# Query and key projections in halves of 512 and 384 tokens, smaller first pieces, and a last tile finished in two halves side by side

## The chip, the cores and the metric

The kernel runs on one core of a Trainium2 chip. The metric is the device time of one execution in microseconds (us), lower is better. The kernel before took 524.78 us (median of 3 runs, 523.88 to 526.72).

## What is computed

One decoder layer on x (8 batches x 112 tokens x 1024 features), in float32: self-attention with 16 heads, cross-attention to a context of 375 rows for each batch, and a linear layer with a low-rank part chosen by batch, each followed by a residual sum and a layer norm.

```python
def reference(x, ctx_4096, Wq, Wk, Wv, Wo, weight, bias, lora_A, lora_B, starts):
    # self-attention: q, k rotated by position, causal mask, softmax, heads of 64
    q, k, v = x @ Wq, x @ Wk, x @ Wv
    x = _layernorm(x + attention(rotary(q), rotary(k), v) @ Wo)
    # cross-attention: one head over the 1024 features
    e = softmax(einsum('bqd,bkd->bqk', x, ctx_4096))
    x = _layernorm(x + einsum('bqk,bkd->bqd', e, ctx_4096))
    # linear layer with a low-rank addition for some batches
    y = einsum('bsd,od->bso', x, weight) + bias
    lo = einsum('bsr,bor->bso', einsum('bsd,brd->bsr', x, A), Bw)
    return _layernorm(x + y + where(use_lora, lo, 0))
```

## The kernel before

The 896 tokens (8 x 112) are seven tiles of 128; the features are eight tiles of 128 (index k). Every large product is made of three: each operand is split into a rounded part (`_hi`, by ScalarE) and the rest (`_lo`, by VectorE or GpSimd), and hi x hi, hi x lo and lo x hi are added up in PSUM. Every engine has one program, written out by hand in order; semaphores tie them together (`then_inc`, `wait_ge`). SyncE (SP) issues nearly all DMAs, in the order of its program.

The stages, in the order of TensorE's program:
- Warm-up: VectorE fills `warm` with ones (L1280), and TensorE multiplies it `WARM_UP` = 4 times (L608). Each of these float32 products stands in the trace as two records.
- Values: L611 to L630. For each k, seven products x_hi x wv_hi, seven x_hi x wv_lo and seven x_lo x wv_hi, one of each for a tile of tokens (L547), into one PSUM bank for each tile. For k = 0 the input comes in pieces: x_feat in columns 0 to 512 and 512 to 896 (L316, L317), the weights from ScalarE's queue (L910). ScalarE rounds x's first piece, the weights, and x's second piece (L979 to L981), VectorE makes the rests (L1292 to L1294).
- Query and key projections with the self-attention: `step` (L584) for each of eight pairs of heads. `project_part` (L534) multiplies the weights of one k (stationary, 128 x 128) with x (moving) for one half h of the tokens, columns 448 h to 448 h + 448, into `PROD[h]`; `project` runs over k. In one step: four k of the query's first half, the scores of the pair before (`score`), its mix with the values (`mix_heads`), the other four k, the query's second half, the key's first half, the key's second half. VectorE's `keep_qk` (L1320) takes each half out of PSUM, four batches at a time, with the rotation's factor (`turn`), and raises `qk_kept`. Between these it masks scores, takes maxima, transposes probabilities (`turn_prob`) and makes rests.
- The output projection `wo`, the cross-attention and the linear layer `ffn` (products of L651, L737, L768 to L773), interleaved tile by tile.
- The normalisations: VectorE measures (`bn_stats`, `bn_aggr`), then `centre` (L1427) writes the variance plus epsilon and the negated mean, each raising `var_set`; GpSimd's `power` (L1738) waits for both, takes the power -0.5 (`rstd_set`), and multiplies it with the negated mean (`shift_set`).
- The end, for the last tile: VectorE measures columns 512 to 1024 straight from PSUM (`measure_y(6, 1)`), GpSimd runs `power`, then VectorE finishes columns 512 to 1024 (L1706) after `rstd_set`, and ScalarE columns 0 to 512 (L1274) after `shift_set`. SyncE stores the two halves one after the other (L522 to L525).

Of the kernel before, what the change touches and what calls it, by code (L numbers as in the profile page):

```python
# [10 lines left out]
ALU = mybir.AluOpType  # L11
ACT = mybir.ActivationFunctionType
AX = mybir.AxisListType

P = 128
# [18 lines left out]
MASKED = -2e9  # L34
WARM_UP = 4
SCORE_SCALE = 1.0 / (2.0 * HD ** 0.5)
# [20 lines left out]
CT_HI = 5  # L57
T_RING = 3
QUAD = 32
QUADS = P // QUAD  # L60
# [47 lines left out]
def tile_of(i):  # L108
    return slice(i * P, i * P + P)
# [13 lines left out]
def build(nc, x_feat, x_tok, qkv_w, wo_w, ffn_w, ctx_feat, ctx_tok, starts, rotary, causal,  # L123
          identity, route, out):
    st = ExitStack()
    with st:
# [3 lines left out]
        def sem(name):  # L130
            return st.enter_context(nc.semaphore(name))
# [110 lines left out]
        wv_in = [[sem(f"wv_in{c}_{k}") for k in range(KT)] for c in range(2)]  # L242
        wv_rounded, wv_rest = sem("wv_rounded"), sem("wv_rest")
        v_done, v_kept = sem("v_done"), sem("v_kept")
        v_in = [sem(f"v_in{c}") for c in range(2)]
# [36 lines left out]
        y_kept, y_stats, y_ready = sem("y_kept"), sem("y_stats"), sem("y_ready")  # L282
        last_ready = [sem(f"last_ready{n}") for n in range(2)]
        y_out = [sem(f"y_out{i}") for i in range(4)]
# [28 lines left out]
        def _(sp):  # L313
            def load_x_feat(k):
                if k == 0:
                    sp.dma_start(x_raw[:, k, 0:HALF], x_feat[:, k, 0:HALF]).then_inc(x_in[k], 16)  # L316
                    sp.dma_start(x_raw[:, k, HALF:B * S], x_feat[:, k, HALF:B * S]  # L317
                                 ).then_inc(x_tail_in, 16)
                else:
                    sp.dma_start(x_raw[:, k, :], x_feat[:, k, :]).then_inc(x_in[k], 16)  # L320
# [200 lines left out]
            i = TILES - 1  # L521
            for n in range(2):  # L522
                sp.wait_ge(last_ready[1 - n], 1)
                cols = slice(HALF * (1 - n), HALF * (1 - n) + HALF)
                sp.dma_start(out_rows[tile_of(i), cols], y_t[i % 4][:, cols]).then_inc(y_out[i % 4], 16)  # L525
            sp.wait_ge(y_out[0], 16 * 2)
# [6 lines left out]
        def _(pe):  # L533
            def project_part(k, w, h, to):  # L534
                for a, b in ((w_hi[w], x_hi), (w_hi[w], x_lo), (w_lo[w], x_hi)):
                    last = pe.matmul(to[:, 0:HT], a[:, k, :], b[:, k, HT * h:HT * h + HT],  # L536
                                     start=(k == 0 and b is x_hi and a is w_hi[w]),
                                     stop=(k == KT - 1 and a is w_lo[w]))
                return last
# [71 lines left out]
            for k in range(KT):  # L611
                pe.wait_ge(x_rounded, k + 2 if k else 1)
                pe.wait_ge(wv_rounded, k + 1)
                for i in range(TILES):
                    if k == 0 and i == HALF // P:
                        pe.wait_ge(x_rounded, 2)
                    value_part(0, k, i, x_hi, wv_hi)
# [291 lines left out]
        def _(act):  # L909
# [68 lines left out]

            round_x(0, slice(0, HALF))  # L979
            round_wv(0, 0)  # L980
            round_x(0, slice(HALF, B * S))  # L981
            for k in range(1, KT):
# [118 lines left out]
            def norm_y(i):  # L1101
# [170 lines left out]
            i = TILES - 1  # L1272
            act.wait_ge(shift_set[2], i + 1)
            act.activation(y_t[i % 4][:, 0:HALF], y_t[i % 4][:, 0:HALF], ACT.Identity,  # L1274
                           bias=norm[2][:, i, 5:6], scale=norm[2][:, i, 4:5]).then_inc(last_ready[0], 1)


        @block.vector
        def _(dve):
# [7 lines left out]
            def rest_x(k, cols=slice(0, B * S)):  # L1287
                dve.wait_ge(x_rounded, k + 2 if k or cols.start else 1)
                dve.tensor_tensor(x_lo[:, k, cols], x_raw[:, k, cols],
                                  x_hi[:, k, cols].bitcast(F32), ALU.subtract).then_inc(x_rest, 1)  # L1290

            rest_wv(0, 0)  # L1292
            rest_x(0, slice(0, HALF))
            rest_x(0, slice(HALF, B * S))  # L1294
            for k in range(1, KT):
# [20 lines left out]

            scale = turn[:, :].unsqueeze(1).broadcast_to([P, HB, S])
            hidden = mask[:, :].unsqueeze(1).broadcast_to([S, HB, S])

            def keep_qk(u, w, h, done, frm):  # L1320
                dve.wait_ge(proj_done, done)
                dve.tensor_tensor(qk[u][w][:, HB * h:HB * h + HB, :],  # L1322
                                  frm[:, 0:HT].rearrange("p (b s) -> p b s", b=HB),
                                  scale, ALU.mult).then_inc(qk_kept, 1)

# [224 lines left out]
            for g in range(3):  # L1550
# [155 lines left out]
            dve.tensor_scalar(y_t[i % 4][:, HALF:D], GROUP[2 * WO - 1][:, :], norm[2][:, i, 0:1],  # L1706
                              norm[2][:, i, 4:5], ALU.subtract, ALU.mult).then_inc(last_ready[1], 1)


        @block.gpsimd  # L1710
        def _(pool):
# [26 lines left out]
            def power(which, i, width):  # L1738
                v = norm[which][0:width, i, :]
                pool.wait_ge(var_set[which], 2 * i + 2)  # L1740
                pool.tensor_tensor(v[:, 4:5], v[:, 2:3], minus_half[0:width, :],  # L1741
                                   ALU.pow).then_inc(rstd_set[which], 1)
                pool.wait_ge(rstd_set[which], i + 1)
                pool.tensor_tensor(v[:, 5:6], v[:, 3:4], v[:, 4:5],
                                   ALU.mult).then_inc(shift_set[which], 1)
# [144 lines left out]
```

## Time and profile before

| | |
|---|---|
| median of 3 runs | 524.78 us (523.88 to 526.72) |
| profiled execution | 525.95 us |
| its span, first to last instruction | 524.2 us |
| mean granted TensorE clock | 0.997 of full speed |
| busy: TensorE products / weight loads | 515.3 us / 444.7 us |
| busy: VectorE / ScalarE / GpSimd | 320.3 / 261.7 / 152.2 us |
| bytes moved by DMA | 65.60 MB, mean 125 GB/s |

PE is TensorE's products, PEld its weight loads (they overlap), DVE is VectorE, ACT ScalarE, POOL GpSimd, SP SyncE. The span of a row is in microseconds from the first instruction. A product's recorded duration overlaps the next product, so the distance of two starts is what one costs in a stream. The granted clock tells at which of its two levels, 1.2 or 2.4 GHz, TensorE runs.

### The profile page before, as it was taken

The page shows a single profiled execution, that of the slowest core. Times are in us where ns is not written, and L with a number is a line of the kernel's source. Part 1 is how long each engine was busy: PE and PEld are TensorE (multiplying, and loading weights), DVE is VectorE, ACT ScalarE, POOL GpSimd, SP SyncE. Part 2 cuts the span into 40 slices and gives each one's busy share as a digit, 9 for nine tenths or more (in the row PEclk, how much of TensorE's full clock was granted, in tenths as well). Part 3 has the DMA queues.
Part 4 walks back from the last instruction along what each step waited for, and adds up shares of the span by engine and source line. Part 5 has one row for each costly group of instructions (what it writes and reads, how often), then busy time and mean ns, then how long its engine had stood idle before and what let it go on. Part 6 is the DMA issues. An engine that isn't in the chain of part 4 may idle for free.

```text
span 524.2 us, 7773 instructions
## 1 busy us (share of the span) xinstructions
PE 515.3 (98%) x2868; PEld 444.7 (85%) x2868; DVE 320.3 (61%) x660; ACT 261.7 (50%) x663; POOL 152.2 (29%) x139
## 2 busy tenths in 40 slices
PE   8999999999999999999999999999998999999995
PEld 5888888999999999999978888888887888988884
DVE  4832000177776868677674797779987776845432
ACT  5713210173846648384565356357777464525231
POOL 0003600436353554642006250114946010110010
PEclk9999999999999999999999999999999999999998
DMA  9906712331112111100087577579986466433011
GB/s 285 314 16 167 195 40 81 107 136 41 41 48 75 42 40 43 41 1 1 1 257 183 138 207 211 148 198 265 274 243 193 126 194 225 109 87 111 2 75 47
DMA packets 37958, 65.60 MB, mean 125 GB/s; under 512 B 4872, under 2 KB 20616, under 8 KB 37920
## 3 DMA queue, kind: packets, MB, share of 16 engines
q1 hardware_dynamic: 37392, 64.84, 42.9%
q8 instruction: 23, 0.38, 0.3%
q10 hardware_dynamic: 528, 0.26, 0.2%
q14 instruction: 15, 0.12, 0.1%
HBM read 54.08 MB, written 3.67 MB: 110 GB/s over the span
## 4 chain that ended last, share of the span: by engine, by line
PE 97%; DVE 2%; issue 0%; ACT 0%; POOL 0%; POOLq 0%; DVEq 0%
PE bank L536 30%; PE bank L651 29%; PE bank L547 15%; PE bank L737 6%; PE bank L563 3%; PE bank L578 3%; PE bank L770 2%; PE bank L768 2%; PE bank L773 2%; PE bank L721 1%; PE bank L609 1%; PE bank L710 1%; PE bank L682 1%; PE bank L684 1%; DVE cf_lo L1506 1%; PE bank L752 0%
## 5 line engine op out<-in xcount | busy, mean ns | idle before, releaser
L536 PE MATMUL bank<-x_hi,w_hi 128*128 128x448 f32 x256 | 94.3, 368 | 0.0
L536 PE MATMUL bank<-x_hi,w_lo 128*128 128x448 f32 x256 | 93.5, 365 | 0.0
L536 PE MATMUL bank<-x_lo,w_hi 128*128 128x448 f32 x256 | 93.5, 365 | 0.0
L1359 DVE STREAM_TRANSPOSE prob_t<-prob 32x256 f32<-32x256 f32 x160 | 69.7, 436 | 13.0 <-ACT prob L942 10.3
L651 PE MATMUL bank<-wo,act_hi 128*128 128x512 f32 x224 | 70.2, 395 | 0.0
L651 PE MATMUL bank<-ffn,act_hi 128*128 128x512 f32 x224 | 69.9, 393 | 0.0
L1728 POOL TENSOR_TENSOR w_lo<-w_mix,w_hi 128x1024 fp32r<-128x1024 f32 x16 | 38.2, 2389 | 105.2 <-ACT w_hi L917 105.2
L932 ACT ACTIVATE prob<-prob,shift 112x112 f32<-112x112 f32 x128 | 47.8, 375 | 38.9 <-DVE shift L1342 38.9
L1741 POOL TENSOR_TENSOR norm<-norm,minus_half 128x1 f32<-128x1 f32 (+1 forms) x22 | 16.6, 754 | 159.9 <-DVE norm L1432 159.9
L536 PEld LDWEIGHTS bank<-x_hi,w_hi 128*128 128x128 f32 x256 | 48.1, 188 | 4.7
L536 PEld LDWEIGHTS bank<-x_hi,w_lo 128*128 128x128 f32 x256 | 48.1, 188 | 3.8
L536 PEld LDWEIGHTS bank<-x_lo,w_hi 128*128 128x128 f32 x256 | 48.1, 188 | 3.7
L651 PEld LDWEIGHTS bank<-wo,act_hi 128*128 128x128 f32 x224 | 41.3, 188 | 8.7
L651 PEld LDWEIGHTS bank<-ffn,act_hi 128*128 128x128 f32 x224 | 41.2, 188 | 8.1
L1028 ACT ACTIVATE ct_hi<-ct_raw 125x512 fp32r<-125x512 f32 x48 | 28.8, 625 | 33.2 <-DMA ct_raw<-ctx_tok 19.8
L917 ACT ACTIVATE w_hi<-w_mix 128x1024 fp32r<-128x1024 f32 x16 | 16.9, 1054 | 54.8 <-PE bank L536 47.0
L651 PE MATMUL bank<-wo,act_lo 128*128 128x512 f32 x112 | 43.7, 390 | 0.0
L651 PE MATMUL bank<-ffn,act_lo 128*128 128x512 f32 x112 | 43.7, 390 | 0.0
L1506 DVE TENSOR_TENSOR cf_lo<-cf_raw,cf_hi 128x752 fp32r<-128x752 f32 x32 | 34.3, 1081 | 7.8 <-ACT cf_hi L1016 7.6
L942 ACT ACTIVATE prob<-prob,inv 112x112 f32<-112x112 f32 x128 | 37.3, 375 | 0.1
L1322 DVE TENSOR_TENSOR q_feat<-bank,turn 128x448 f32<-128x448 f32 x16 | 9.9, 619 | 43.4 <-PE bank L536 43.3
L1499 DVE TENSOR_TENSOR ct_lo<-ct_raw,ct_hi 125x512 fp32r<-125x512 f32 x48 | 32.9, 719 | 5.4 <-ACT ct_hi L1028 5.1
(114 smaller groups left out, 984.1 us busy)
## 6 DMA issues: line engine op xcount, KB each, us to landing
cf_raw<-ctx_feat SPq DMA_DIRECT2D x32, 376.0 KB, 4.3
ct_raw<-ctx_tok SPq DMA_DIRECT2D x24, 448.0 KB
w_raw<-qkv_w SPq DMA_DIRECT2D x16, 512.0 KB, 3.4
half_raw<-wo_w SPq DMA_DIRECT2D x16, 256.0 KB, 6.0
half_raw<-ffn_w SPq DMA_DIRECT2D x16, 256.0 KB, 6.1
wv_raw<-qkv_w SPq DMA_DIRECT2D x15, 256.0 KB, 7.5
x_raw<-x_feat SPq DMA_DIRECT2D x7, 448.0 KB, 8.2
out<-y_t SPq DMA_DIRECT2D x6, 512.0 KB, 3.6
```

What stands on the lines that cost most here:

```text
L536: last = pe.matmul(to[:, 0:HT], a[:, k, :], b[:, k, HT * h:HT * h + HT], start=(k == 0 and b is x_hi and a is w_hi[w]), stop=(k == KT - 1 ...
L547: return pe.matmul(value_bank(c, i)[:, :], a[:, k, tile_of(i)], w[c][:, k, :], start=(k == 0 and a is x_hi and w is wv_hi), stop=(k == KT ...
L651: last = pe.matmul(to[:, :], a[:, k, cols], weight(of, n, k, w), start=(k == 0 and a is act_hi and w == 0), stop=(ends and k == KT - 1 and ...
L737: last = pe.matmul(CSCORE[0:S, 0:LKP], a[:, k, tokens_of(b)], c[slot][:, kk, :], start=(k == 0 and a is act_hi and c is cf_hi), stop=(k == ...
L917: act.activation(w_hi[w][:, :, :], w_mix[:, :, :], ACT.Copy).then_inc(w_rounded, 1)
L932: last = act.activation(prob[a][:, b, :], prob[a][:, b, :], ACT.Exp, bias=shift[:, a, b:b + 1], accum_out=total[:, a, b:b + 1])
L942: last = act.activation(prob[a][:, b, :], prob[a][:, b, :], ACT.Copy, scale=inv[:, a, b:b + 1])
L1028: act.activation(ct_hi[m % CT_HI][:, :], ct_raw[c][:, HALF * n:HALF * n + HALF], ACT.Copy).then_inc(ct_rounded, 1)
L1359: return dve.transpose(quads(prob_t_wide[r], key, query), quads(prob_wide[r], query, key))
L1499: dve.tensor_tensor(ct_lo[c][:, cols], ct_raw[c][:, cols], ct_hi[m % CT_HI][:, :].bitcast(F32), ALU.subtract).then_inc(ct_rest[n], 1)
L1506: dve.tensor_tensor(cf_lo[slot][:, :, :], cf_raw[slot][:, :, :], cf_hi[slot][:, :, :].bitcast(F32), ALU.subtract).then_inc(cf_rest, 1)
L1728: pool.tensor_tensor(w_lo[w][:, :, :], w_mix[:, :, :], w_hi[w][:, :, :].bitcast(F32), ALU.subtract).then_inc(w_rest, 1)
```

## The change

It has three parts.
1. `project_part` splits the tokens at SPLIT = 512 instead of 448: the first half is 512 columns wide, the second 384. As 512 is four batches and 64 tokens, `keep_qk` uses two instructions for a half: one for the part of batch 4 that the half holds (64 or 48 columns), one for the whole batches (4 or 3).
2. `WARM_UP` is 2. The first load of x is split at FIRST = 256 tokens instead of 512. ScalarE rounds columns 0 to 256 of the first piece of value weights, VectorE copies columns 256 to 512 with the same rounding (`wv_tail_rounded`), and TensorE waits for both.
3. In the last tile ScalarE centres columns 0 to 512 as soon as the negated mean is there, scales them after `rstd_set`, and issues their store from its own queue; SyncE stores columns 512 to 1024. In every normalisation `power` starts its first instruction after the variance, and waits for the negated mean only ahead of the second.

```diff
-WARM_UP = 4
+WARM_UP = 2
+FIRST = 2 * P
+SPLIT = HB * S + 64
...
-                    sp.dma_start(x_raw[:, k, 0:HALF], x_feat[:, k, 0:HALF]).then_inc(x_in[k], 16)
-                    sp.dma_start(x_raw[:, k, HALF:B * S], x_feat[:, k, HALF:B * S]
+                    sp.dma_start(x_raw[:, k, 0:FIRST], x_feat[:, k, 0:FIRST]).then_inc(x_in[k], 16)
+                    sp.dma_start(x_raw[:, k, FIRST:B * S], x_feat[:, k, FIRST:B * S]
...
-            for n in range(2):
-                sp.wait_ge(last_ready[1 - n], 1)
-                cols = slice(HALF * (1 - n), HALF * (1 - n) + HALF)
-                sp.dma_start(out_rows[tile_of(i), cols], y_t[i % 4][:, cols]).then_inc(y_out[i % 4], 16)
+            sp.wait_ge(last_ready, 1)
+            sp.dma_start(out_rows[tile_of(i), HALF:D], y_t[i % 4][:, HALF:D]).then_inc(y_out[i % 4], 16)
...
             def project_part(k, w, h, to):
+                cols = slice(SPLIT * h, SPLIT + (B * S - SPLIT) * h)
                 for a, b in ((w_hi[w], x_hi), (w_hi[w], x_lo), (w_lo[w], x_hi)):
-                    last = pe.matmul(to[:, 0:HT], a[:, k, :], b[:, k, HT * h:HT * h + HT],
+                    last = pe.matmul(to[:, 0:cols.stop - cols.start], a[:, k, :], b[:, k, cols],
...
                 pe.wait_ge(wv_rounded, k + 1)
+                if k == 0:
+                    pe.wait_ge(wv_tail_rounded, 1)
                 for i in range(TILES):
-                    if k == 0 and i == HALF // P:
+                    if k == 0 and i == FIRST // P:
                         pe.wait_ge(x_rounded, 2)
...
-            round_x(0, slice(0, HALF))
-            round_wv(0, 0)
-            round_x(0, slice(HALF, B * S))
+            round_x(0, slice(0, FIRST))
+            act.wait_ge(wv_in[0][0], 16)
+            act.activation(wv_hi[0][:, 0, 0:FIRST], wv_raw[0][:, 0, 0:FIRST],
+                           ACT.Copy).then_inc(wv_rounded, 1)
+            round_x(0, slice(FIRST, B * S))
...
-            act.wait_ge(shift_set[2], i + 1)
+            act.wait_ge(var_set[2], 2 * i + 2)
             act.activation(y_t[i % 4][:, 0:HALF], y_t[i % 4][:, 0:HALF], ACT.Identity,
-                           bias=norm[2][:, i, 5:6], scale=norm[2][:, i, 4:5]).then_inc(last_ready[0], 1)
+                           bias=norm[2][:, i, 3:4], scale=1.0).then_inc(last_centred, 1)
+            act.wait_ge(rstd_set[2], i + 1)
+            act.wait_ge(last_centred, 1)
+            act.activation(y_t[i % 4][:, 0:HALF], y_t[i % 4][:, 0:HALF], ACT.Copy,
+                           scale=norm[2][:, i, 4:5]).then_inc(last_scaled, 1)
+            act.wait_ge(last_scaled, 1)
+            act.dma_start(out_rows[tile_of(i), 0:HALF], y_t[i % 4][:, 0:HALF]).then_inc(y_out[i % 4], 16)
...
+            dve.wait_ge(wv_in[0][0], 16)
+            dve.tensor_copy(wv_hi[0][:, 0, FIRST:HALF], wv_raw[0][:, 0, FIRST:HALF]
+                            ).then_inc(wv_tail_rounded, 1)
+            dve.wait_ge(wv_tail_rounded, 1)
             rest_wv(0, 0)
-            rest_x(0, slice(0, HALF))
-            rest_x(0, slice(HALF, B * S))
+            rest_x(0, slice(0, FIRST))
+            rest_x(0, slice(FIRST, B * S))
...
             def keep_qk(u, w, h, done, frm):
                 dve.wait_ge(proj_done, done)
-                dve.tensor_tensor(qk[u][w][:, HB * h:HB * h + HB, :],
-                                  frm[:, 0:HT].rearrange("p (b s) -> p b s", b=HB),
-                                  scale, ALU.mult).then_inc(qk_kept, 1)
+                first = SPLIT - HT
+                if h == 0:
+                    whole, at_whole = slice(0, HB), 0
+                    some, at_some = slice(0, first), HT
+                else:
+                    whole, at_whole = slice(HB + 1, B), S - first
+                    some, at_some = slice(first, S), 0
+                n, m = whole.stop - whole.start, some.stop - some.start
+                dve.tensor_tensor(qk[u][w][:, HB, some], frm[:, at_some:at_some + m],
+                                  turn[:, some], ALU.mult)
+                dve.tensor_tensor(qk[u][w][:, whole, :],
+                                  frm[:, at_whole:at_whole + n * S].rearrange("p (b s) -> p b s", b=n),
+                                  turn[:, :].unsqueeze(1).broadcast_to([P, n, S]),
+                                  ALU.mult).then_inc(qk_kept, 1)
...
-                pool.wait_ge(var_set[which], 2 * i + 2)
+                pool.wait_ge(var_set[which], 2 * i + 1)
                 pool.tensor_tensor(v[:, 4:5], v[:, 2:3], minus_half[0:width, :],
                                    ALU.pow).then_inc(rstd_set[which], 1)
+                pool.wait_ge(var_set[which], 2 * i + 2)
                 pool.wait_ge(rstd_set[which], i + 1)
```

## Rows read from the trace of the kernel before

**Rows 1.** The page, busy time, share of the span and instructions of TensorE.

```profile
PE 515.3 (98%) x2868; PEld 444.7 (85%) x2868; DVE 320.3 (61%) x660; ACT 261.7 (50%) x663; POOL 152.2 (29%) x139
```

**Rows 2.** The chain that ended last, from 0 to 20 us: start, length, what.

```profile
1.38 5.47 PE bank L609 x8
```

**Rows 3.** Waits of TensorE, whole span: us in total, times, longest.

```profile
PE bank L682 <- DVE t_both L1530: 1.5, 1, 1.5
```

**Rows 4.** Timeline of TensorE in a projection step: start us, duration, what.

```profile
176.63 0.37 PE L536 MATMUL bank<-x_hi,w_hi 128*128 128x448 f32 x1
...
186.77 0.37 PE L536 MATMUL bank<-x_hi,w_lo 128*128 128x448 f32 x1
```

**Rows 5.** Timeline in the value stage, seven products merged to one row.

```profile
11.50 1.75 PE L547 MATMUL bank<-wv_hi,x_hi 128*128 128x512 f32 x7
...
16.26 1.75 PE L547 MATMUL bank<-wv_hi,x_hi 128*128 128x512 f32 x7
```

**Rows 6.** Timeline of TensorE in the cross scores.

```profile
309.15 0.33 PE L737 MATMUL bank<-cf_hi,act_lo 128*112 128x376 f32 x1
...
312.56 0.33 PE L737 MATMUL bank<-cf_lo,act_hi 128*112 128x376 f32 x1
```

**Rows 7.** Timeline of TensorE in the low-rank products.

```profile
446.32 0.28 PE L791 MATMUL bank<-act_hi,a_both 128*112 128x256 f32 x1
...
447.72 0.28 PE L791 MATMUL bank<-act_hi,a_both 128*112 128x256 f32 x1
```

**Rows 8.** Weight loads by line and shape: busy us, mean ns, idle before.

```profile
L536 PEld LDWEIGHTS bank<-x_hi,w_hi 128*128 128x128 f32 x256 | 48.1, 188 | 4.7
...
L737 PEld LDWEIGHTS bank<-cf_hi,act_hi 128*112 128x112 f32 x64 | 11.2, 174 | 0.3
```

**Rows 9.** Timeline of VectorE at a step's end, and two short instructions.

```profile
193.26 0.62 DVE L1322 TENSOR_TENSOR k_feat<-bank,turn 128x448 f32<-128x448 f32 x1 [1.97 <-PE bank L536]
...
196.66 1.16 DVE L1334 SCALAR_TENSOR_TENSOR prob<-bank,mask 112x448 f32<-112x448 f32 x2 [0.50 <-PE bank L563]
...
404.65 0.47 DVE L1530 SCALAR_TENSOR_TENSOR t_both<-bank,sel,t_both 48x112 fp32r<-48x112 f32 x2
```

**Rows 10.** Timeline of all engines at the start.

```profile
4.53 0.34 PEld L609 LDWEIGHTS bank<-warm 128*128 128x128 f32 x1 [0.41 <-issue]
4.94 0.63 ACT L921 ACTIVATE wv_hi<-wv_raw 128x512 fp32r<-128x512 f32 x1 [0.16 <-DMA wv_raw<-qkv_w]
...
5.28 0.34 PEld L609 LDWEIGHTS bank<-warm 128*128 128x128 f32 x1 [0.41 <-issue]
5.48 0.51 ACT L970 ACTIVATE x_hi<-x_raw 128x384 fp32r<-128x384 f32 x1
...
5.94 0.19 PEld L609 LDWEIGHTS bank<-warm 128*128 128x128 f32 x1 [0.32 <-issue]
...
6.69 1.34 PEld L547 LDWEIGHTS bank<-wv_hi,x_hi 128*128 128x128 f32 x6 [0.19 <-issue]
...
9.01 0.62 ACT L921 ACTIVATE wv_hi<-wv_raw 128x512 fp32r<-128x512 f32 x1
```

**Rows 11.** Timeline of the other engines behind the last product.

```profile
519.18 0.15 DVE L1431 TENSOR_SCALAR norm<-norm 128x1 f32<-128x1 f32 x1
519.25 0.14 DVE L1432 TENSOR_SCALAR norm<-norm 128x1 f32<-128x1 f32 x1
519.47 0.55 POOL L1741 TENSOR_TENSOR norm<-norm,minus_half 128x1 f32<-128x1 f32 x1 [11.65 <-DVE norm L1432]
520.06 0.81 DVE L1706 TENSOR_SCALAR y_t<-bank,norm 128x512 f32<-128x512 f32 x1 [0.66 <-POOL norm L1741]
...
520.33 0.81 ACT L1274 ACTIVATE y_t<-y_t,norm 128x512 f32<-128x512 f32 x1 [7.42 <-POOL norm L1744]
520.89 0.81 SPq L525 DMA_DIRECT2D out<-y_t  x2
```

**Rows 12.** DMA issues from 505 us on: KB each, median us to landing.

```profile
out<-y_t SPq DMA_DIRECT2D x2, 256.0 KB, 2.2
```

More of the change, by code:

```diff
@@ L243, in build @@
         wv_rounded, wv_rest = sem("wv_rounded"), sem("wv_rest")
+        wv_tail_rounded = sem("wv_tail_rounded")
         v_done, v_kept = sem("v_done"), sem("v_kept")
@@ L282, in build @@
         y_kept, y_stats, y_ready = sem("y_kept"), sem("y_stats"), sem("y_ready")
-        last_ready = [sem(f"last_ready{n}") for n in range(2)]
+        last_centred, last_scaled, last_ready = sem("last_centred"), sem("last_scaled"), sem("last_ready")
         y_out = [sem(f"y_out{i}") for i in range(4)]
@@ L1315, in _ @@
                               ALU.is_equal).then_inc(routed, 1)
-            scale = turn[:, :].unsqueeze(1).broadcast_to([P, HB, S])
             hidden = mask[:, :].unsqueeze(1).broadcast_to([S, HB, S])
@@ L1706, in _ @@
             dve.tensor_scalar(y_t[i % 4][:, HALF:D], GROUP[2 * WO - 1][:, :], norm[2][:, i, 0:1],
-                              norm[2][:, i, 4:5], ALU.subtract, ALU.mult).then_inc(last_ready[1], 1)
+                              norm[2][:, i, 4:5], ALU.subtract, ALU.mult).then_inc(last_ready, 1)
         @block.gpsimd
```

## The prediction

> **What bounds the kernel now.** I read the busy table of the page first: TensorE is busy 98% of the span [rows 1]. The chain of work that ended last says the same in order of time: it is TensorE from its first warm-up product at 1.38 us [rows 2] up to the end, where VectorE's last statistics follow it. The table of waits names one stall of TensorE after the start, 1.5 us for VectorE in the feed-forward part [rows 3]. So a change shortens the kernel by what it takes off TensorE's own stream, by what it takes off the start ahead of that stream, and by what it takes off the chain behind it. Everything else is cover. The profiled execution took 525.95 us (span 524.2 and 1.75 around it), 1.2 us over the median of the runs, 524.78; I sum on the profile and subtract the result from the median.
>
> **Part 1, the projections.** The number of products stays 768: 8 pairs of heads x 2 matrices x 8 feature tiles x 3 products x 2 halves. Before, both halves are 448 tokens wide; after, 384 products are 512 wide and 384 are 384 wide. The columns in all are the same, so the question is how the spacing of two products depends on the width. The traced duration of one product (365 ns) overlaps its neighbour, so I take starts. 448 wide: 50 products from 176.63 to 186.77 us, 202.8 ns each [rows 4]. 512 wide, same 128-column weights: 21 products from 11.50 to 16.26 us, 226.7 ns each [rows 5]. 376 wide, weights of 112 columns: 20 from 309.15 to 312.56 us, 170.5 ns each [rows 6]. 256 wide, weights of 64 and 112 columns in turn: 12 from 446.32 to 447.72 us, 116.7 ns each [rows 7].
>
> Per column that is 0.448 ns from 256 to 376, 0.449 ns from 376 to 448, and only 0.373 ns from 448 to 512. The line bends at the top: the last 64 columns are cheaper than the ones before. A 384-wide product isn't in the trace; its nearest row is the 376-wide one, so I take 170.5 + 8 x 0.449 = 174.1 ns. A pair then costs 226.7 + 174.1 = 400.8 ns instead of 2 x 202.8 = 405.6 ns, and 384 pairs give 384 x -4.8 ns = **-1.8 us**. Bounds: if 384 columns cost their share of 512 (170.0 ns) the term is -3.4 us. If the slope of 0.373 also holds below 448, 384 columns cost 178.9 ns and the term is 0. Above nothing there is the weight load: its record lasts 188 ns for 128 columns and 174 ns for 112 [rows 8]. If the next product had to wait for the end of that record, a 384-wide one would be spaced at 188 ns at least, 384 x +9.1 ns = +3.5 us, and at up to the 202.8 ns of now, +9.2 us. Against such a floor: the 376-wide products run at 170.5 ns though their weight load is recorded with 174 ns, and the 256-wide ones at 116.7 ns with loads of up to 112 columns [rows 6, 7]. So the record holds latency that overlaps, and 16 more weight columns, 14 ns more, don't make a floor of 188.
>
> The Trainium skill speaks against this gain. TensorE: Matmul & The Clock Gate, Back-to-back issue gap, has a gap of N columns at 2.4 GHz plus about 2.5 ns, the weights loading meanwhile; by that the pair costs 378.4 ns both ways and part 1 is worth nothing. The trace is above it at each width (202.8 and 226.7 ns against 189.2 and 215.8), by 13.6 ns at 448 and 10.9 ns at 512.
>
> Moved with it: VectorE now keeps each half with two instructions, for 448 + 64 and 48 + 336 columns, the short ones some 0.24 us (nearest: 48x112, two in 0.47 us) [rows 9]. There are 32 short ones, and as each of the 16 pairs of halves goes from 2 x 0.62 to about 1.5 us, VectorE has 16 x 0.3 = 5 us more. Cover: VectorE is idle 1.97 us before the last keep of a step, and 0.50 us before the masking of the next scores [rows 9]; the latter is the tight one. There the second half is now the narrow one (0.7 us against 0.62), and TensorE's twelve products ahead of the scores are wider (12 x 23.9 ns = 0.29 us later), so the slack grows. TensorE's other waits on a kept half stand a whole half (4.2 us) behind its end. Queued behind a keep on VectorE are the transposes of the probabilities, which come 0.1 us later. I cost all this at nothing; without that cover it is 0.1 us a step, +0.8 us.
>
> **Part 2, the start.** Before, TensorE doesn't get to the first value product at its readiness. ScalarE rounds the first weight piece from 4.94 us for 0.63 us, so its data are there at 5.57, but eight warm-up records (two per product) hold the engine: the chain passes to the value products at 1.38 + 5.47 = 6.85 us [rows 2, 10]. The records are 0.75 us apart while the clock is at its lower level (1.2 GHz, weight load 0.34 us), the one of 5.28 us comes 0.66 us before the next and the one of 5.94 us has a load of 0.19 us: the clock rose at about 5.85 us, to 2.4 GHz [rows 10]. After: four records, so TensorE is free at about 4.55 us. Rounding costs 0.63 us for 512 columns and 0.51 for 384 [rows 10], so 0.39 us for 256; ScalarE's half is ready at 4.94 + 0.39 = 5.33 and VectorE copies the other half beside it (its nearest row is 0.62 us for 448 columns [rows 9], so an estimate of 0.3 to 0.5 us for 256 and an end at 5.3 to 5.4). Products start at about 5.4 us. Until 5.85 us they run at the lower level, which wastes 0.23 us; 0.16 us is the lag that the chain's 6.85 has too (its weight loads go on from 6.69 [rows 10]). The third token tile needs the rest of x rounded: ScalarE starts it at about 5.4 and needs 0.73 us for 640 columns, 6.15 us, which stalls about 0.1 us. So the take-over of the chain moves to 5.4 + 0.23 + 0.16 + 0.1 = 5.9 us: **-0.95 us**. Next limit: the second feature tile's weights are rounded at 9.01 + 0.62 = 9.63 us [rows 10]; TensorE asks for them after 21 products, at about 10.5 us, so 0.9 us of cover remain. The first load in two other pieces (256 and 640 columns for 512 and 384) moves the same bytes, and what lands last ahead of TensorE is the weight piece, which is as before. Bounds: -1.3 us if the piece also lands earlier, -0.5 us if VectorE's copy is late.
>
> The engine is now idle from 4.55 to 5.4 us ahead of the rise of the clock. No row shows whether the rise still comes at 5.85 then; that is rival C.
>
> **Part 3, the end.** Behind the last product stand VectorE's statistics, two small instructions, GpSimd's power (0.55 us) and product, then both engines' half of the last tile, and two stores of SyncE, 0.41 us apart [rows 11]. Now: ScalarE's half is ready at 520.33 + 0.81 = 521.14, its store issued at about 521.3 us and landed 2.2 us later [rows 11, 12]. After: GpSimd starts on the first small instruction (end 519.33 for 519.39, -0.07 us). ScalarE centres from 519.45 to 520.26, beside the power, and scales with 0.81 us from 520.3 to 521.1; its store goes out on its own queue at 521.15. VectorE's half ends at 520.80 and SyncE stores it at once. The later issue moves from 521.3 to 521.15: **-0.15 us**. Bounds: -0.4 us if scaling alone is shorter, +0.3 us if a store from ScalarE's queue lands later than one from SyncE's. The earlier power in the other normalisations is off TensorE's path: nothing.
>
> Sum: -1.8 - 0.95 - 0.15 = -2.9 us: 523.05 us for the profiled execution, **521.9 us** for the median (0.55% less).
>
> **The rivals.**
> A, forecast, 0.55: as summed, 521.9 us; with the bounds of its terms all at once (-3.4 to 0, -1.3 to -0.5, -0.4 to +0.3) 519.7 to 524.6 us.
> B, 0.15: the widths are worth nothing, because cost is linear from 384 to 512 columns; the skill's gap rule ends here too. For it: the slope of 0.373 is the only one measured with 128-column weights at both ends. Against it: two other intervals agree on 0.449. Only the start and end remain, -1.1 us: 523.7 us.
> C, 0.17: the clock rises later, because the engine is idle ahead of it. For it: in the trace the rise came after 4.5 us of unbroken work. Against: only 0.85 us are idle, and TensorE is at work again when the rise was. If the break makes the count begin anew, the rise comes 4.5 us after 5.4, at 9.9 instead of 5.85 us; 4.05 us at half speed cost 2.0 us: -2.9 + 2.0 = -0.9 us, 523.9 us. The Trainium skill (TensorE: Matmul & The Clock Gate, The HAM clock gate) says that the lower level is the default and that sustained activity releases it; what a short break does there, no row of this case shows.
> D, the slower side, 0.09: the weight load sets a floor under the narrow products. It decides from a floor of 181.8 ns on (at 178.9 ns part 1 is even, and 2.9 ns more, 384 times, eat the 1.1 us of parts 2 and 3). At 188 ns the sum is +3.5 - 1.1 = +2.4 us, 527.2 us; at 202.8 ns +9.2 - 1.1 = +8.1 us, 532.9 us.
> E, 0.04: the gain of the first parts is lost again where TensorE waits 1.5 us for VectorE [rows 3]. The wait ends a run of VectorE work that itself begins when TensorE's cross products of batch 3 end (add_row waits for them), so it should move along with TensorE. If the wait grew by half its length, 0.8 us would go, and if by its length 1.5 us: 522.7 to 523.4 us.
>
> **Range and chances.** About 0.5% (2.6 us) is what a measurement of this kernel can tell from no change; the forecast is just beyond it. A lies beyond with seven tenths of its chance (0.39) and inside with the rest; B, C and E lie inside but for some scatter of the measurement, and D lies inside at a floor of 188 ns (527.2 us is 0.46% more) and beyond it above. So: faster by over 0.5% 0.41, within 0.5% 0.52, slower 0.07. The range reaches from A's low bounds taken nearly together, 520.3 us, over B, C and E with their scatter, to 524.9 us, and leaves out D and what is beyond A's low end.
>
> **What the profile after would show.** Part 1: starts of 384-wide products 174 ns apart (B: 179; D: 188 or more) and of 512-wide ones 227 ns, and a step (48 pairs) 0.23 us shorter; VectorE's idle time before the masking not under 0.5 us, no new wait of TensorE on the kept halves. Part 2: four warm-up records, the first value product at 5.4 us, the second feature tile's at 10.5 us instead of 11.50; the change of spacing from 0.43 to 0.23 us tells when the clock rose, and C is right if that is later than 6 us. Part 3: the store of ScalarE's queue at 521.15 on the old time axis. What would make this wrong: a 384-wide spacing away from 174 ns, a late rise of the clock, or a new wait in the projection steps.

## The result, and the profile after

The kernel after takes 523.08 us (median of 22 runs, 522.11 to 527.09) against 525.07 us for the kernel before in the same sessions (22 runs). The two medians differ by 2.0 us. The ratio of the two kernels is 0.9968, with a 95% interval from 0.9957 to 0.9979; by it, the kernel takes 1.7 us less, between 1.1 and 2.3. The forecast was 2.9 us less, 521.9 us, with a range of 520.3 to 524.9 us.

The profiled execution of after took 522.58 us, its span is 520.6 us. That is 3.6 us below the span of before, nearly twice the difference of the medians, so the two traces alone mislead; e1 below shows by how much. The page of after, its span and busy times (compare rows 1):

```profile
span 520.6 us, 7823 instructions
...
PE 513.0 (99%) x2864; PEld 438.4 (84%) x2864; DVE 319.8 (61%) x693; ACT 262.6 (50%) x664; POOL 152.1 (29%) x139
```

Four product records less (two warm-up products), 33 VectorE instructions more. The start, from the timeline of all engines of after (compare rows 10):

```profile
1.38 3.36 PE L612 MATMUL bank<-warm 128*128 128x448 f32 x4 [1.38 <-DVE warm L1293]
...
3.18 0.42 ACT L975 ACTIVATE x_hi<-x_raw 128x256 fp32r<-128x256 f32 x1 [0.67 <-DMA x_raw<-x_feat]
...
3.97 0.42 ACT L986 ACTIVATE wv_hi<-wv_raw 128x256 fp32r<-128x256 f32 x1 [0.38 <-DMA wv_raw<-qkv_w]
3.97 0.29 DVE L1306 CAST wv_hi<-wv_raw 128x256 fp32r<-128x256 f32 x1 [2.65 <-DMA wv_raw<-qkv_w]
...
4.49 0.84 PE L550 MATMUL bank<-wv_hi,x_hi 128*128 128x512 f32 x2
...
4.79 0.74 ACT L975 ACTIVATE x_hi<-x_raw 128x640 fp32r<-128x640 f32 x1 [0.40 <-DMA x_raw<-x_feat]
...
5.58 1.43 PE L550 MATMUL bank<-wv_hi,x_hi 128*128 128x512 f32 x5 [0.25 <-ACT x_hi L975]
...
10.01 1.75 PE L550 MATMUL bank<-wv_hi,x_hi 128*128 128x512 f32 x7
```

The first value product starts at 4.49 us, not at the forecast 5.4, because the weight piece itself is there at 3.97 instead of 4.94 us. TensorE waits 0.25 us for the rest of x; the forecast had 0.1. The second feature tile begins at 10.01 us instead of 11.50 [rows 5].

The projections, from TensorE's timeline in the third step, two places where the width changes (compare rows 4):

```profile
131.18 0.33 PE L539 MATMUL bank<-x_hi,w_hi 128*128 128x384 f32 x1
...
132.25 0.34 PE L539 MATMUL bank<-x_hi,w_hi 128*128 128x384 f32 x1
...
133.11 0.33 PE L539 MATMUL bank<-x_hi,w_lo 128*128 128x384 f32 x1
...
135.19 0.33 PE L539 MATMUL bank<-x_hi,w_lo 128*128 128x384 f32 x1
135.37 0.39 PE L539 MATMUL bank<-x_hi,w_hi 128*128 128x512 f32 x1
...
137.45 0.39 PE L539 MATMUL bank<-x_hi,w_hi 128*128 128x512 f32 x1
137.67 0.39 PE L539 MATMUL bank<-x_lo,w_hi 128*128 128x512 f32 x1
...
140.39 0.39 PE L539 MATMUL bank<-x_lo,w_hi 128*128 128x512 f32 x1
```

A settled narrow stream costs (135.19 - 133.11) / 12 = 173.3 ns a product, a settled wide one (140.39 - 137.67) / 12 = 226.7 ns. But the first six behind a change to 384 columns cost (132.25 - 131.18) / 6 = 178 ns, and the first nine behind a change to 512 cost (137.45 - 135.37) / 9 = 231 ns. Over the stage the means are 174.4 and 228.9 ns, 403.3 ns a pair against 405.3 before. Left out of these means are 14 spacings in each kernel (292 to 310 ns before, 317 to 339 ns after), where TensorE passes from a projection to the scores or goes on after them. The whole stage, from the first product of the projections to the first of the output projection, runs from 81.41 to 260.07 us:

```profile
81.41 0.39 PE L539 MATMUL bank<-x_hi,w_hi 128*128 128x512 f32 x1
...
260.07 0.63 PE L656 MATMUL bank<-wo,act_hi 128*128 128x512 f32 x2
```

That is 178.66 us; before, the same two records stand at 82.90 and 262.36 us, 179.46. In nanoseconds the differences are 178,652 and 179,459, and each of the other traces with the same widths and order repeats its number to the nanosecond (e2, e7, e8, e10 and e12 the one of after; e1, e3, e4 and e9 the one of before). So this stage is worth 0.81 us, and nothing of it is scatter.

VectorE's cover held. The end of a step in its timeline (compare rows 9):

```profile
191.25 0.21 DVE L1346 TENSOR_TENSOR k_feat<-bank,turn 128x48 f32<-128x48 f32 x1 [1.15 <-PE bank L539]
191.37 0.50 DVE L1348 TENSOR_TENSOR k_feat<-bank,turn 128x336 f32<-128x336 f32 x1
191.90 2.24 DVE L1386 STREAM_TRANSPOSE prob_t<-prob 32x256 f32<-32x256 f32 x5
194.97 1.16 DVE L1361 SCALAR_TENSOR_TENSOR prob<-bank,mask 112x448 f32<-112x448 f32 x2 [0.83 <-PE bank L566]
```

The idle time before the masking grew from 0.50 to 0.83 us. All keeps together take 22.0 us instead of 19.9, 2.1 us more, where the prediction had 5.

### The profile page after: what moved, and what is told of

It is laid out like the page before. It is cut to its first block, busy times and chain, and to the rows that moved or that the text cites. A ratio compares the mean times of both kernels' runs of the same rounds, so it can differ in the third digit from the quotient of the medians.

```text
span 520.6 us, 7823 instructions
## 1 busy us (share of the span) xinstructions
PE 513.0 (99%) x2864; PEld 438.4 (84%) x2864; DVE 319.8 (61%) x693; ACT 262.6 (50%) x664; POOL 152.1 (29%) x139
## 4 chain that ended last, share of the span: by engine, by line
PE 98%; DMA 1%; ACT 0%; DVE 0%; SPq 0%; issue 0%; ACTq 0%
PE bank L539 30%; PE bank L656 30%; PE bank L550 15%; PE bank L742 6%; PE bank L566 3%; PE bank L581 3%; PE bank L773 2%; PE bank L775 2%; PE bank L778 2%; PE bank L726 1%; PE bank L715 1%; DMA x_raw<-x_feat 1%; PE bank L687 1%; PE bank L793 1%; PE bank L689 1%; PE bank L796 1%
## 5 line engine op out<-in xcount | busy, mean ns | idle before, releaser
L539 PE MATMUL bank<-x_hi,w_hi 128*128 128x512 f32 (+1 forms) x256 | 93.7, 366 | 0.0
L539 PE MATMUL bank<-x_hi,w_lo 128*128 128x512 f32 (+1 forms) x256 | 93.2, 364 | 0.0
L539 PE MATMUL bank<-x_lo,w_hi 128*128 128x512 f32 (+1 forms) x256 | 93.1, 364 | 0.0
L550 PE MATMUL bank<-wv_hi,x_hi 128*128 128x512 f32 x112 | 36.3, 393 | 0.2 <-ACT x_hi L975 0.2
L1533 DVE TENSOR_TENSOR cf_lo<-cf_raw,cf_hi 128x752 fp32r<-128x752 f32 x32 | 30.9, 979 | 8.1 <-ACT cf_hi L1023 8.1
```

The lines of the kernel that those rows point to most:

```text
L539: last = pe.matmul(to[:, 0:cols.stop - cols.start], a[:, k, :], b[:, k, cols], start=(k == 0 and b is x_hi and a is w_hi[w]), stop=(k == K ...
L550: return pe.matmul(value_bank(c, i)[:, :], a[:, k, tile_of(i)], w[c][:, k, :], start=(k == 0 and a is x_hi and w is wv_hi), stop=(k == KT ...
L1533: dve.tensor_tensor(cf_lo[slot][:, :, :], cf_raw[slot][:, :, :], cf_hi[slot][:, :, :].bitcast(F32), ALU.subtract).then_inc(cf_rest, 1)
```

## The experiments

Each edit is against the kernel before or after, as named. Ratios are to the kernel before, with their 95% intervals; 0.001 is 0.52 us.

**e1, the kernel before again.** No edit.

> The kernel before once more, for a second trace. In the first one TensorE waited 1.5 us for t_both at 403.6 us, behind one 128x752 subtraction of VectorE (cf_lo) that lasted 3.12 us instead of 0.94, with a GpSimd subtraction running beside it; after the change the wait was gone and TensorE 1.5 us further ahead. Theory 1 (accident of phase between VectorE and GpSimd): the second trace shows another length there, and the 1.5 us are not the change's. Theory 2 (fixed by the program): 3.1 us and a wait of 1.5 us again. Also open: the first weight piece was there at 4.94 us before and at 3.97 after. If that is scatter of the DMA, this trace shows another time than 4.94; if the larger pieces cause it, 4.9 again.

Measured: span 521.9 us, 2.3 us less than the first trace of the same kernel. TensorE has no wait at 403 us, and the subtraction is as short as its kind. Its VectorE row, and GpSimd's rows around it:

```profile
400.07 0.93 DVE L1506 TENSOR_TENSOR cf_lo<-cf_raw,cf_hi 128x752 fp32r<-128x752 f32 x1
...
401.01 2.54 POOL L1757 TENSOR_TENSOR ffn<-half_raw,ffn 128x512 fp32r<-128x512 f32 x2
```

In the first trace of before the order of the two is turned: GpSimd's pair of subtractions starts at 400.36 us, VectorE's at 400.58, and VectorE's lasts 3.12 us. It ends at 403.70 us, 0.80 us after the end of GpSimd's pair (402.90):

```profile
400.36 2.54 POOL L1757 TENSOR_TENSOR ffn<-half_raw,ffn 128x512 fp32r<-128x512 f32 x2
...
400.58 3.12 DVE L1506 TENSOR_TENSOR cf_lo<-cf_raw,cf_hi 128x752 fp32r<-128x752 f32 x1
```

Two later traces, e6 and e12, show a third outcome. This is e6:

```profile
398.58 3.25 POOL L1785 TENSOR_TENSOR ffn<-half_raw,ffn 128x512 fp32r<-128x512 f32 x2
...
398.74 1.93 DVE L1533 TENSOR_TENSOR cf_lo<-cf_raw,cf_hi 128x752 fp32r<-128x752 f32 x1
```

Here VectorE gets in between the two: it ends 0.80 us after GpSimd's first subtraction (399.87), and GpSimd's second takes 2.00 us instead of 1.29. In e12 VectorE's takes 2.08 us, again ending 0.80 us after GpSimd's first, and GpSimd's second 1.99 us. So the one that comes second waits for the end of the other's instruction. The Trainium skill (SBUF — State Buffer, SBUF: two separate sides) says this of a VectorE instruction with two SBUF inputs and a GpSimd instruction that reads SBUF: an exclusive lock on a shared port pair for the whole instruction, no sharing. The traces agree: 0.93 us with VectorE first, 1.93 us behind one subtraction of GpSimd, 3.12 us behind two. Why VectorE gets in between the two in e6 and e12 and not in before and e4 is open. Theory 1 holds: the length is an accident of phase. From the first product of the output projection to the last product of all it is 255.42 us in the first trace of before, 253.73 in e1 and 254.22 in after: 1.2 of the 3.6 us between the two spans lie in a stretch that moves by 1.7 us with no edit at all. The weight piece is rounded from 4.98 us here (4.94 before), so its time isn't scatter of that size.

**e2, the widths alone.** Before, with the projections and keeps of after:

```diff
+SPLIT = HB * S + 64
-                    last = pe.matmul(to[:, 0:HT], a[:, k, :], b[:, k, HT * h:HT * h + HT],
+                    last = pe.matmul(to[:, 0:cols.stop - cols.start], a[:, k, :], b[:, k, cols],
```

> Only the projections in 512 and 384 columns. Prediction on record: -1.8 us. From the trace of after: 384-wide products settle at 173.3 ns and 512-wide ones at 226.7, but the first ten or so behind each change of width or of kind are spaced wider (231 ns on average for the wide ones), so a pair costs 403.3 instead of 405.3 ns: 384 x -2.0 = -0.8 us. Rival: the widths are worth nothing, 0 us.

Measured: 0.9995 (0.9978 to 1.0012), 524.42 us. The time alone can't tell -0.8 us from 0. The trace can: the stage takes 178.65 us again (83.14 to 261.79), 0.81 us less than the two traces of before.

**e3, the start alone.** Before, with the warm-up, pieces and split rounding of after:

```diff
-WARM_UP = 4
+WARM_UP = 2
+FIRST = 2 * P
-            round_x(0, slice(0, HALF))
-            round_wv(0, 0)
+            round_x(0, slice(0, FIRST))
+            act.activation(wv_hi[0][:, 0, 0:FIRST], wv_raw[0][:, 0, 0:FIRST],
+                           ACT.Copy).then_inc(wv_rounded, 1)
```

> Only the start: smaller first pieces, two warm-up products, the weight piece rounded by two engines. Prediction on record -0.95 us; the two traces show -1.48 us up to the second feature tile, of which 0.97 us is an earlier landing of the weight piece. If that landing is the change's, -1.5 us; if it is scatter, -0.9 us; if the clock often rises late, between 0 and -0.5 us with more scatter than before.

Measured: 0.9974 (0.9963 to 0.9986), 1.4 us less (0.7 to 1.9). The weight piece lands early here too:

```profile
3.37 0.42 ACT L974 ACTIVATE x_hi<-x_raw 128x256 fp32r<-128x256 f32 x1 [0.86 <-DMA x_raw<-x_feat]
4.19 0.42 ACT L985 ACTIVATE wv_hi<-wv_raw 128x256 fp32r<-128x256 f32 x1 [0.40 <-DMA wv_raw<-qkv_w]
```

So the landing is the change's: the smaller first piece of x is followed by an earlier weight piece, though that comes from another queue. ScalarE begins on it at 4.87 to 5.25 us in the six traces with the old pieces, and at 3.95 to 4.21 us in the eight with the new ones. The first piece of x itself lands at 4.11 to 4.42 us with the old pieces and at 3.16 to 3.36 us with the new ones, and the weight piece lands 0.73 to 0.84 us behind it in all 14. No run changed the size of the pieces alone, but e7 and e8 rule out the number of warm-up products as the cause.

**e4, the end alone.** Before, with the last tile and `power` of after:

```diff
-            act.wait_ge(shift_set[2], i + 1)
+            act.wait_ge(var_set[2], 2 * i + 2)
+            act.dma_start(out_rows[tile_of(i), 0:HALF], y_t[i % 4][:, 0:HALF]).then_inc(y_out[i % 4], 16)
-                pool.wait_ge(var_set[which], 2 * i + 2)
+                pool.wait_ge(var_set[which], 2 * i + 1)
```

> Only the end: halves side by side, store from ScalarE's queue, power a step earlier. Prediction -0.15 us; the traces show the end of the last half at 3.17 us behind the last product's start against 3.37 before, so -0.2 to -0.3 us. Rival: a store from ScalarE's queue lands later and eats it, 0 us.

Measured: 1.0003 (0.9991 to 1.0015). In the traces the last byte's landing stands 5.75 us behind the start of the last product with the new end (e4 and after) and 5.84 us with the old one (before and e1; e3 has 5.82): 0.09 us less, below what the timing can see. This trace again has the long subtraction (3.35 us) and a wait of 1.7 us for t_both.

**e5, halves of 480 and 416.** Before, with the widths' code and another SPLIT:

```diff
+SPLIT = HB * S + 32
```

> The kernel before with halves of 480 and 416 columns, for their spacing. Theory 1: a settled stream costs the width at 2.4 GHz plus 13.3 ns (512: 226.7, 384: 173.3), and 448 is the odd one that never settles (202.7 instead of 200.0). Then 480 settles at 213.3 ns and 416 at 186.7 ns, 400.0 ns a pair, as 512 and 384 do, each with ten or so wider spacings behind a change. Theory 2: the line bends between 448 and 512 as the prediction had it: 480 at 214.7 and 416 at 188.4 ns, in every spacing.

Measured: from TensorE's timeline of one step:

```profile
135.16 0.35 PE L539 MATMUL bank<-x_hi,w_lo 128*128 128x416 f32 x1
...
137.40 0.35 PE L539 MATMUL bank<-x_hi,w_lo 128*128 128x416 f32 x1
...
139.11 0.38 PE L539 MATMUL bank<-x_lo,w_hi 128*128 128x480 f32 x1
...
142.57 0.38 PE L539 MATMUL bank<-x_hi,w_lo 128*128 128x480 f32 x1
```

2.24 us / 12 = 186.7 ns for 416 columns, 3.46 us / 16 = 216.3 ns for 480 (217.1 on average over the stage). Theory 1 is right for 416 and wrong for 480; theory 2 is wrong for both. Theory 1 also has ten or so wider spacings behind a change of width, and these don't come: the mean of all 384 spacings of 416 columns is 186.8 ns, the settled value. The unsettled spacings are thus seen at 384 and 512 columns, and not at 416. The stage takes 178.92 us, 0.54 us less than with 448.

This trace also shows that the long subtraction isn't the only thing that delays t_both. TensorE waits 1.0 us for it, though VectorE's subtraction takes 0.94 us; VectorE then waits for ScalarE, which itself had waited for a DMA:

```profile
400.52 0.84 ACT L1019 ACTIVATE cf_hi<-cf_raw 128x752 fp32r<-128x752 f32 x1 [1.36 <-DMA cf_raw<-ctx_feat]
...
403.71 0.42 DVE L1529 TENSOR_TENSOR bank<-bank,t_part 48x256 f32<-48x256 f32 x1 [1.38 <-ACT t_part L1089]
```

In e8 it is the same, with a wait of TensorE of 0.8 us.

**e6, narrow behind narrow, wide behind wide.** After, with the key's halves in the other order (their banks, keeps and the scores' wait go with them):

```diff
-                project(1, 0, PROD[0])
+                project(1, 1, PROD[0])
                 pe.wait_ge(qk_kept, 4 * s + 2)
-                project(1, 1, PROD[1])
+                project(1, 0, PROD[1])
```

> The kernel after, with the key's narrow half ahead of its wide half, so that wide follows wide and narrow follows narrow, and the width changes twice a step less. Theory 1: the unsettled spacings behind a change of width are what ate half of the gain: 40 ns behind a change to 512 and 26 ns behind one to 384, 66 ns less in each step, 0.5 us less than after, 0.9958 of before. Theory 2: they follow something else (the start of an accumulation, the kept half), and nothing moves: 0.9968.

Measured: 0.9956 (0.9943 to 0.997), 522.97 us. The stage runs from 81.41 to 259.57 us, 178.16 us: 0.49 us less than after, against 0.5 expected.

```profile
81.41 0.39 PE L539 MATMUL bank<-x_hi,w_hi 128*128 128x512 f32 x1
...
259.57 0.62 PE L656 MATMUL bank<-wo,act_hi 128*128 128x512 f32 x2
```

Theory 1 holds: the unsettled spacings follow the change of width. The evidence is the trace; in time alone the interval overlaps with that of after.

**e7, four warm-up products again.** After, with

```diff
-WARM_UP = 2
+WARM_UP = 4
```

> The kernel after with four warm-up products instead of two. Theory 1: they hold the engine while the operands wait: the first value product goes from 4.5 back to between 5.7 and 6.9 us, according to when the clock rises; 0.9 to 1.2 us more than after, 0.999 of before. Theory 2: the earlier pieces alone make the gain at the start, and it stays at 0.997.

Measured: 0.9976 (0.9963 to 0.9989), 523.9 us. The second feature tile begins at 11.36 us, 1.35 us later than in after, with the clock rising at 5.55 against 4.79 us. In time it is 0.4 us more than after, and the intervals overlap; the direction is theory 1's, the size is smaller than expected, and the time alone doesn't show it. At the second feature tile the earlier pieces without the shorter warm-up bring 0.14 us against before (11.36 for 11.50 us), and the clock's earlier rise in that trace (5.55 for 5.84 us) can account for them. The eight records still hold the engine:

```profile
1.38 5.32 PE L612 MATMUL bank<-warm 128*128 128x448 f32 x8 [1.38 <-DVE warm L1293]
6.20 2.13 PE L550 MATMUL bank<-wv_hi,x_hi 128*128 128x512 f32 x7
```

**e8, no warm-up.** After, with

```diff
-WARM_UP = 2
+WARM_UP = 0
```

> The kernel after without a warm-up. If the rise of the clock wants work before it, it comes later than in any run so far (4.8 to 7.3 us) and the value stage starts at the lower level: up to 1.5 us more than after, 0.999 or so. Rival: the clock rises when it did, and nothing moves, 0.9968.

Measured: 0.9983 (0.9972 to 0.9993), 524.09 us. By the ratios that is 0.8 us more than after, and the intervals overlap a little (0.9972 and 0.9979).

```profile
4.76 3.26 PE L550 MATMUL bank<-wv_hi,x_hi 128*128 128x512 f32 x7 [4.76 <-ACT wv_hi L986]
7.86 1.76 PE L550 MATMUL bank<-wv_lo,x_hi 128*128 128x512 f32 x7
...
11.04 1.75 PE L550 MATMUL bank<-wv_hi,x_hi 128*128 128x512 f32 x7
```

The first seven products take 3.26 us, nearly twice what a settled seven take (1.75): they run at 1.2 GHz. The clock rose at 7.68 us, in this one trace 0.27 us later than in the latest of the others (4.66 to 7.41). The second feature tile begins at 11.04 us, within the range of the traces with two warm-up products (9.99 to 11.10), so this trace doesn't show where the 0.8 us are lost.

**e9 and e10, the masking of the low-rank part ahead of the long subtraction.** Before (e9) and after (e10), with

```diff
             rest_turned("a5")
-            rest_cf(22)
             mask_t(0)
+            rest_cf(22)
```

> The kernel before with VectorE's mask_t(0), for which TensorE waits at 403 us, ahead of the subtraction of the context chunk 22 (which in two traces of four lasted over 2 us beside GpSimd). Theory 1: that wait (0 to 2.1 us, another in each trace) is an accident of phase behind a long subtraction; with the order turned it is gone, the median falls by about 1 us (0.998) and the scatter of the runs shrinks. Theory 2: VectorE's total work up to there sets it, and the wait comes back one place later (cross_score of batch 5 for its chunk): 1.000.

Measured: 0.9996 (0.9984 to 1.0007). In the trace the wait of TensorE for t_both is gone and none has come in its place: the last product starts 253.65 us after the first of the output projection, against 255.42 us in the first trace of before and 253.73 us in e1. The median doesn't fall, and the scatter of the runs doesn't shrink (523.40 to 526.17 us; before 523.67 to 526.34). So neither theory holds as written: the accident is real in a single execution, but the median of before seems to hold little of it.

> The kernel after with the same turned order. Theory 1: 0.5 to 1 us less than after, 0.995 to 0.996 of before, with the ratio to the previous kernel of this call equal to the sum of the parts (start -1.4, widths -0.8, end -0.1 us: 0.9956). Theory 2: as after, 0.9968.

Measured: 0.9972 (0.9961 to 0.9984), 523.5 us; no wait in this trace either. Theory 2: as after.

**e11, both.** The edits of e6 and e10 together.

> The kernel after with both: the key's narrow half first and mask_t(0) first. If the two are independent: after -0.5 us -0.7 us, 0.9945 of before, the fastest so far. If the wider shift only brings other collisions of VectorE with GpSimd: 0.9956, as with the swap alone.

Measured: 0.9954 (0.9941 to 0.9966), 522.11 us, the fastest of the study, and no faster than the swap alone within its interval.

**e12, both stores from SyncE.** After, with

```diff
             sp.dma_start(out_rows[tile_of(i), HALF:D], y_t[i % 4][:, HALF:D]).then_inc(y_out[i % 4], 16)
+            sp.wait_ge(last_scaled, 1)
+            sp.dma_start(out_rows[tile_of(i), 0:HALF], y_t[i % 4][:, 0:HALF]).then_inc(y_out[i % 4], 16)
...
-            act.wait_ge(last_scaled, 1)
-            act.dma_start(out_rows[tile_of(i), 0:HALF], y_t[i % 4][:, 0:HALF]).then_inc(y_out[i % 4], 16)
```

> The kernel after, with both stores of the last tile from SyncE's queue again (the halves still side by side). The store from ScalarE's queue was issued at 517.50 us and landed 2.5 us later, while SyncE's landed 2.0 us after 517.34. Theory 1: ScalarE's queue is the slower one; from SyncE the second store is issued 0.35 us behind the first, at 517.7, and lands after 2.2 us, so the end is the same within 0.1 us. Theory 2: two stores in flight slow one another whatever their queue: the second lands 2.5 us after its issue, and the end comes 0.2 us later.

Measured: the end is where theory 1 has it, but that doesn't make its reason right. The last landing is 5.74 us behind the last product's start, as in after (5.75). The table of DMA issues of after and of e12 (KB each, median us to landing):

```profile
out<-y_t SPq DMA_DIRECT2D x1, 256.0 KB, 2.0
out<-y_t ACTq DMA_DIRECT2D x1, 256.0 KB, 2.5
```

```profile
out<-y_t SPq DMA_DIRECT2D x2, 256.0 KB, 2.2
```

The second store is issued 0.16 us behind the first from ScalarE's queue and takes 2.53 us; from SyncE's queue it is issued 0.38 us behind and takes 2.31 us. Both land 2.69 us after the issue of the first store. In all 14 traces the last landing stands 2.69 to 2.73 us behind that first issue, whatever the queue and the moment of the second. So the end follows the first store, and the queue of the second makes no difference to it; whether a queue is slower in itself, these runs can't tell.

## Why the prediction was right, and which of its terms were off

The time is a sum of four stretches, and the traces give each on its own:

| | forecast | in the traces | timed alone |
|---|---|---|---|
| start, to the second feature tile | -0.95 us | -1.4 us (means of six) | -1.4 (-1.9 to -0.7) |
| projections | -1.8 us | -0.81 us | -0.3 (-1.2 to +0.6) |
| after them, to the last product | 0 | scatter, 253.65 to 255.76 us | |
| behind the last product | -0.15 us | -0.09 us | +0.2 (-0.5 to +0.8) |
| sum | -2.9 us | -2.3 us | |

Sign and range held, and luck had a part in it: the two large terms were off in opposite directions, the projections by 1.0 us too much and the start by 0.5 us too little. The sum of the traces is at the edge of the measured interval (-1.1 to -2.3); the 0.6 us between it and the 1.7 us by the ratio stay open (0.3 us against the medians). Two stretches vary between traces of the same code: the start, with the moment at which the clock rises, and the stretch after the projections, where e9 and e10 didn't settle it.

Part 1, the step that failed: "a pair then costs 226.7 + 174.1". The interpolated 174.1 ns was right (174.4 on average), though for a reason the prediction didn't have. What was mis-sized is the 226.7 ns, which I read from a stream that had been 512 wide for a long time. In a step the width changes four times, and six to nine unsettled spacings follow each change, so the mean is 228.9 ns; 384 x (403.3 - 405.3) = -0.8 us. The trace of before could have warned me: its six spacings of value products from 6.92 to 8.31 us, behind the change from the 448-wide warm-up, are 231 ns each on average, ahead of the settled 226.7. e6 shows the mechanism by taking two of the four changes away: the 0.49 us come back.

Part 2, the step that failed: "what lands last ahead of TensorE is the weight piece, which is as before". It landed 0.97 us earlier, and the bound for that (-1.3 us) was taken too near. The forecast start of the value products, 5.4 us, became 4.49 us in after. The second feature tile begins at 10.36 us on average in the six traces with the new start and two warm-up products (9.99 to 11.10), and at 11.77 us in the six with the old one (10.89 to 12.25). In the same traces the clock rose 0.5 us earlier on average with the new start (5.87 against 6.40 us); at half a microsecond for each, some 0.2 us of the 1.4 us go with that (an estimate), and six traces of each can't tell whether it is chance.

Part 3: right in sign and too small to be timed. The step that failed is "The later issue moves from 521.3 to 521.15". On the time axis of before it moved further, from 521.27 to 520.99 us, but the landing doesn't follow the later issue: it follows the first one, which moved by 0.06 us, from 3.12 to 3.06 us behind the start of the last product. The 2.2 us to landing that the term used is the median of two stores; the later one took 2.34 us, and they are 0.38 us apart, not 0.41.

The rivals.

B (widths worth nothing) falls by the 0.81 us that repeat in every trace. The gap rule of the Trainium skill (TensorE: Matmul & The Clock Gate, Back-to-back issue gap), which the page gives for an isolated product, doesn't describe these streams: 384 columns cost 173.3 ns settled against 162.5 by the rule, and the pair is 5.3 ns cheaper when both are settled, not the same.

C (the clock rises late after the break) wasn't put to the test. Over six traces each, the rise comes at 4.66 to 7.36 us with the old start and at 4.79 to 7.41 us with the new one, with no later middle. But the condition of C never arose: as the weight piece landed earlier, the break of 0.85 us that I had worked out shrank to almost nothing (the fourth warm-up record would give way at about 4.53 us, the first value product is recorded at 4.49), and only the 0.25 us at 5.58 remain. What a break of 0.85 us would do, no run tried. e8, with no work before the value products, has the latest rise, but by a margin of 0.27 us in a single trace. Each microsecond of a later rise costs a little under half of one at the second feature tile (after: 4.79 and 10.01 us; e10: 7.41 and 11.10 us).

D (a floor from the weight load) falls: products of 384 columns with 128-column loads are 173.3 ns apart.

E (the wait at 403 us grows) was right that this wait is free to move, and doesn't say what moves it: in before and e4 (1.5 and 1.7 us), and less in e6 and e12 (0.3 and 0.5 us), VectorE's subtraction stands behind GpSimd's; in e5 and e8 (1.0 and 0.8 us) no subtraction is long, and ScalarE's part comes late behind a DMA. After has no such wait.

## What to carry to other kernels

Price a product by the distance of starts, by width, and in the surroundings it will have: at 384 and 512 columns a settled stream is cheaper than the six to nine products behind each change of width, so group equal widths, and measure the pair that you have, for at 416 nothing of it was seen. Trim a warm-up to what fits ahead of the first operands; taking it away altogether gained nothing here (0.8 us more by the ratios, with intervals that overlap a little). And before you give two traces' difference to an edit, profile the same kernel twice: here one collision of VectorE with GpSimd went with 1.7 us of difference between two traces of one kernel, more than the largest part of the change.

## What the runs showed that I had not expected

The cost of a product above its width at 2.4 GHz isn't monotonic: settled, 13.3 ns at 384 and 512 columns, 13.4 at 416, but 16.0 at 448 and 16.3 at 480 (over 12 to 50 products each, all with 128-column weights). A pair of 512 and 384 costs 400.0 ns settled, two of 448 cost 405.3. Why 448 and 480 are dearer is open; no run here tells it.

A smaller first transfer on one queue brought another queue's first transfer forward: it lands at 3.93 to 4.18 us instead of 4.84 to 5.23, with the same bytes asked for. By 3 us of the span 0.29 MB have moved in after and 0.12 MB in before. Why is open.
